# A quarter of a graph network's column terms from bf16 matmuls over runs of sorted edges instead of an indirect gather

## The reference

```python
for l in range(N_LAYERS):                      # 3
    f1 = relu(x[row] @ nb_W[l] + nb_b[l])
    f2 = relu(x[col] @ self_W[l] + self_b[l])
    h = relu(concatenate([f1, f2], axis=1) @ att1_W[l] + att1_b[l])
    log_alpha = (h @ att2_W[l] + att2_b[l])[:, 0]
    mask = clip(sigmoid(log_alpha) * (ZETA - GAMMA) + GAMMA, 0.0, 1.0)
    rowsum = segment_sum(mask, row, num_segments=n) + 1e-06
    d_inv_sqrt = clip(rowsum ** (-0.5), 0.0, 10.0)
    vals = mask * d_inv_sqrt[row] * d_inv_sqrt[col]
    x = segment_sum(vals[:, None] * x[col], row, num_segments=n)
    out = out + x
return layernorm(x_in + out)
```

## Time and profile before

| | us |
|---|---|
| median of 3 runs | 12785.2 |
| lowest, highest | 12784.3, 12812.13 |
| span of the profiled execution | 9111.0 |
| attention stage of one layer (669 to 2740) | 2071 |
| weight stage of one layer (2800 to 3425) | 625 |

### The profile page before, as it was taken

One profiled execution on the slowest core, in us unless ns is written; L12 is line 12 of the kernel. 1 busy time (PEld: TensorE's weight loads), 2 busy tenths in 40 slices (PEclk: granted clock), 3 DMA queues, 4 the chain that ended last, 5 costly groups with the idle time before them and its releaser, 6 DMA issues.

```text
span 9111.0 us, 203370 instructions
## 1 busy us (share of the span) xinstructions
PE 5650.8 (62%) x43467; PEld 5151.5 (57%) x43630; DVE 6736.5 (74%) x29039; ACT 3666.1 (40%) x8663; POOL 5960.7 (65%) x6294
## 2 busy tenths in 40 slices
PE   3135555555558996555555557998555555555996
PEld 1135555545548885555555556887555555555886
DVE  8877777777777877777777777877777777776788
ACT  0013322322227883322322325885322322323886
POOL 0017777777775656777777776665777777776664
PEclk7565555555558996555555557998555555555998
DMA  1014444444456664444444446665444444445665
GB/s 24 0 48 135 132 130 131 132 130 130 133 128 206 213 206 130 132 131 130 132 130 131 132 130 176 210 212 156 132 130 130 133 130 131 132 130 146 213 211 161
DMA packets 1122388, 1272.27 MB, mean 140 GB/s; under 512 B 648596, under 2 KB 652724, under 8 KB 1122356
## 3 DMA queue, kind: packets, MB, share of 16 engines
q1 hardware_dynamic: 922676, 903.51, 32.1%
q0 software_dynamic: 199680, 368.45, 16.7%
HBM read 868.11 MB, written 403.23 MB: 140 GB/s over the span
## 4 chain that ended last, share of the span: by engine, by line
POOL 44%; issue 23%; PE 22%; DVE 8%; DMA 1%; ACT 1%; POOLq 0%; DVEq 0%; ACTq 0%; SPq 0%
POOL got L526 22%; PE bank L552 12%; POOL k_hot L526 11%; POOL g_hot L526 10%; PE bank L685 6%; DVE acc L946 2%; DVE acc L947 2%; PE bank L653 1%; PE bank L690 1%; PE bank L610 1%; PE bank L601 1%; PE bank L576 1%; DMA k_x<-kept_x 1%; DMA k_hot<-qx_table,index 0%; DVE acc L909 0%
## 5 line engine op out<-in xcount | busy, mean ns | idle before, releaser
L653 PE MATMUL bank<-p_all,onehot_t 128*128 x10032 | 2301.5, 424 | 1752.4 <-issue 1731.8
L653 PEld LDWEIGHTS bank<-p_all,onehot_t 128*128 128x128 f32 x10032 | 2186.8, 330 | 1803.4 <-issue 1803.4
L526 POOL DMA_INDIRECT got<-qx_table,index x2496 | 2376.4, 952 | 784.9 <-issue 780.3
L539 POOL DMA_INDIRECT got<-y_table,index x1248 | 1187.3, 951 | 798.8 <-issue 431.5
L798 ACT ACTIVATE small<-small 128x8 f32<-128x8 f32 x624 | 130.2, 209 | 3813.9 <-DVE small L1080 3813.9
L526 POOL DMA_INDIRECT k_hot<-qx_table,index x1248 | 1181.3, 947 | 393.7 <-issue 377.5
L526 POOL DMA_INDIRECT g_hot<-qx_table,index x1248 | 1185.6, 950 | 380.6 <-issue 380.6
L552 PE MATMUL bank<-mask,onehots 128*128 128x3 bf16 x4992 | 669.8, 184 | 986.1 <-DVE mask L1091 986.1
L552 PEld LDWEIGHTS bank<-mask,onehots 128*128 128x128 bf16 x4992 | 516.0, 104 | 1250.7 <-issue 1145.5
L1118 DVE SCALAR_TENSOR_TENSOR p_all<-iota_b,col_hi,bank 128x104 f32<-128x104 bf16 x3768 | 953.9, 317 | 341.5 <-PE bank L685 335.4
L1056 DVE TENSOR_SCALAR onehots<-iota_b,rows_b 128x128 bf16<-128x128 bf16 x5016 | 888.7, 280 | 48.0
(11 more groups left out here) (167 smaller groups left out, 8859.7 us busy)
## 6 DMA issues: line engine op xcount, KB each, us to landing
onehot_t<-look_hot SPq DMA_DIRECT2D x474, 256.0 KB
row_hot<-onehots SPq DMA_DIRECT2D x468, 256.0 KB, 3.6
k_x<-col_rows SPq DMA_DIRECT2D x318, 256.0 KB, 3.6
kept_x<-got SPq DMA_DIRECT2D x312, 256.0 KB
look_hot<-k_x SPq DMA_DIRECT2D x312, 256.0 KB, 2.1
hot_in<-row_hot SPq DMA_DIRECT2D x312, 256.0 KB
k_x<-kept_x SPq DMA_DIRECT2D x312, 256.0 KB
look_new<-row_hot SPq DMA_DIRECT2D x159, 256.0 KB
```

The lines of the kernel that those rows point to most:

```text
L526: pool.indirect_dma_start(got[j][:, k, :], None, qx_table, bass.IndirectOffsetOnAxis(ap=index[j][:, k:k + 1], axis=0)).then_inc(a_got[j], 16)
L539: pool.indirect_dma_start(got[j][:, k, 0:HID], None, y_table, bass.IndirectOffsetOnAxis(ap=index[j][:, k:k + 1], axis=0)).then_inc(g_got[j ...
L653: last = mm(bank_p[h][:, k, :], onehot_t[h][:, k, :], p_all[:, ds(ids[k], 1), :].rearrange("p o d -> p (o d)"), start=True, stop=True)
```

## The change

One group in four, j = 3 of each quad, no longer gathers q. All edges are sorted by column too (the key is now block, column, row), so that a tile is a few runs of edges from the same column block, and for each run a bf16 one-hot over 128 columns times the block of q gives all of the run's terms. q is kept as three bf16 parts (`q3`, in the storage of `acc`) whose sum is q, so that a product has 192 columns. A quad has 72 such run slots: 9 rounds of 8. A round's one-hot is 128x1024 bf16; the rounds r % 3 < 2 are made by DVE in one compare (`build_slots`), every third by ACT in two activations (`make_third`). Two buffers hold them, `slot_hot[r % 2]`, and a buffer is free when PE has used the round two before (`x_used`). SP broadcasts each round's lane numbers from DRAM, 256 KB, into one of three buffers.

```diff
 # SP, quad loop
+                        if j == 0:
+                            sp.wait_ge(x_used[0], l * (slots_used(0) * QUADS) + b * slots_used(0))
+                            sp.dma_start(slot_word[0:1, :], slot_words[ds(b, 1), 1, :]).then_inc(w_in, 16)
+                            for r in range(3):
+                                load_slots(b, r, 0 if r == 0 else None)
...
+                        if j < 2:
+                            for r in (3 * j + 3, 3 * j + 4):
+                                load_slots(b, r, r - 2)          # waits until round r - 3 is made
...                                                               # kept_x store, look_hot store (waits a_look[j])
+                        if j < 2:
+                            load_slots(b, 3 * j + 5, 3 * j + 3)
 # POOL, quad loop: 3 groups in place of 4
-                    for j in range(4):
+                    for j in range(3):
...
+                pool.memset(acc[:, :, :], 0.0).then_inc(k_zero, 1)   # was 14 ACT copies per layer
 # PE
+                def column_terms(b, j):
...
+                    for r in range(3 * j, 3 * j + 3):
+                        pe.load(q_at + k_at, slot_word[0:1, 2 * U * r:2 * U * (r + 1)])   # 16 int32 registers
+                        pe.wait_ge(*slots_made(l, b, r))
+                        for i in range(U):
+                            of = pe.snap(q_at[i], min_val=0, max_val=(NB - 1) * Q_COLS)
+                            to = pe.snap(k_at[i], min_val=0, max_val=(U - 1) * OUT_COLS)
+                            last = plus(bank_q[:, ds(to, Q_COLS)], slot_hot[r % 2][:, i * PARTS:(i + 1) * PARTS],
+                                        q3_flat[:, ds(of, Q_COLS)])
+                        last.then_inc(x_used[r % 2], 1)
+                    for j in range(4):
+                        g = b * 4 + j
+                        if j == 2:
+                            column_terms(b, j)
+                            row_terms(1, g + 1)                  # into the same banks as the column terms
+                        else:
+                            row_terms(1 - j % 2, g + 1, a_sum, l * GROUPS + g)
+                        turn_hot((j + 2) % 4, g + 2)
+                        if j == 0:
+                            pe.wait_ge(a_sum, l * GROUPS + g)
+                            for i in range(4):
+                                clear(bank[4 + i])
+                        if j < 2:
+                            column_terms(b, j)
...                                                               # then the row sums, as before
 # ACT
+                def make_third(b, j):
+                    third, h, n = 3 * j + 2, j % 2, l * (3 * QUADS) + (b * 3 + (j + 1))
+                    act.wait_ge(x_in[2], n * 16)
+                    a.activation(slot_in[2], slot_in[2], ACT.Abs, bias=minus_part[:, :]).then_inc(x_away, 1)
+                    act.wait_ge(x_used[h], l * (slots_used(h) * QUADS) + (b * slots_used(h) + third // 2))
+                    act.wait_ge(x_away, n)
+                    a.activation(slot_hot[h], slot_in[2], ACT.Relu, bias=one[:, :], scale=-1.0).then_inc(x_third, 1)
                         a.activation(small[j % 2][:, 1, :], small[j % 2][:, 7, :], ACT.Exp, scale=-1.0).then_inc(a_sig, 1)
+                        if j == 2:
+                            make_third(b, j)
                         keep_turned(j % 2, g + 2, g + 1)
                         if j < 3:
                             make_look(b, j)
+                        if j < 2:
+                            make_third(b, j)
 # DVE
+                def build_slots(b, r):
+                    h = r % 2
+                    dve.wait_ge(x_in[r % 3], ...)
+                    dve.wait_ge(x_used[h], l * (slots_used(h) * QUADS) + (b * slots_used(h) + r // 2))
+                    v.tensor_scalar(slot_hot[h], slot_in[r % 3], part_f[:, :], None, ALU.is_equal).then_inc(x_made, 1)
-                        build_hot(hot_a[h], ...)                 # cast, 8 compares
+                        if j < 3:
+                            build_slots(b, 3 * j)
+                            build_slots(b, 3 * j + 1)
+                        build_hot((j + 2) % 4, g + 2, g, b + (j >= 2))   # one build_onehot of 128x1024, bf16
                         dve.wait_ge(a_p, l * (GROUPS + 1) + (g + 1))
-                        v.tensor_tensor(bank_p[h], bank_p[h], got[j][:, :, 0:HID], ALU.add)
+                        # j < 3: the same add; j == 3:
+                            v.tensor_reduce(terms, q_parts[:, :, 0:Q_COLS].rearrange("p k (s d) -> p k d s", s=PARTS_OF),
+                                            AX.X, ALU.add).then_inc(a_parts, 1)
-                        build_hot(hot_b[1 - h], ...)             # the second set of row one-hots
 # DVE, give_columns, per node step
+                    v.tensor_copy(q3[:, of_step(s), 0, :], q_out).then_inc(q_hi, 1)
+                    v.tensor_tensor(q_rest[j], q_out, q3[:, of_step(s), 0, :], ALU.subtract).then_inc(q_left, 1)
 # ACT: a copy per node step (split_middle); POOL: q3 part 2 = q_rest - q3 part 1
```

More of the change, by code:

```diff
@@ L206, in build @@
         onehots = sb("onehots", [PARTS, 4 * U, PARTS], BF16)
-        hot_a, hot_b = ([onehots[:, h * U:(h + 1) * U, :] for h in (first, first + 1)] for first in (0, 2))
+        hot = [onehots[:, j * U:(j + 1) * U, :] for j in range(4)]
         onehot_t = ring("onehot_t", [PARTS, U, PARTS], F32)
@@ L212, in build @@
                   .rearrange("p (k m) -> p k m", m=PARTS) for c in range(3)]
[L213 removed]
+        index = [sb(f"index{h}", [PARTS, U], I32) for h in range(3)]
         hidden = ring("hidden", [PARTS, U, HID], F32)
@@ L574, in _ @@
                 of = keys[stages_before(n) % 2]
+                if n == TURNS - 1:
+                    pe.wait_ge(s_ranked, 1)
+                    for h in range(2):
+                        last = turn(bank[7][:, h * PARTS:(h + 1) * PARTS], other[:, h * PARTS:(h + 1) * PARTS], ident_f[:, :])
+                    last.then_inc(s_kk, 1)
+                    of = other
+                    pe.wait_ge(s_perm, 16)
+                    pe.wait_ge(s_lo, 1)
                 for c in range(COLS // PARTS):
@@ L985, in _ @@
                     n += 1
-            done, free = keys[n % 2].bitcast(I32), keys[(n + 1) % 2].bitcast(I32)
-            link(v.tensor_scalar(free, done, PARTS - 1, None, ALU.bitwise_and))
-            v.tensor_copy(col_lo, free).then_inc(s_lo, 1)
+            done, moved = sorted_of.bitcast(I32), other.bitcast(I32)
+            own, real, group_key, runs, rank, first, rest, few, kk = (ranks[:, k, :] for k in range(9))
+            link(v.tensor_scalar(moved, done, HI_AT, None, ALU.logical_shift_right))
@@ new lines, in _ @@
+            link(v.tensor_tensor(starts[:, 1:COLS], moved[:, 1:COLS], moved[:, 0:COLS - 1], ALU.not_equal))
+            link(v.memset(starts.rearrange("p (t e) -> p t e", e=PARTS)[:, :, 0:1], 1.0))
+            link(v.tensor_reduce(runs, starts.rearrange("p (h e) -> p h e", h=2), AX.X, ALU.add))
+            link(v.scalar_tensor_tensor(out=kk, in0=runs, scalar=float(ALL_GROUPS), in1=group_key, op0=ALU.mult, op1=ALU.add))
+            v.tensor_copy(other[:, 0:ALL_GROUPS].rearrange("p (h m) -> p h m", h=2),
+                          kk.unsqueeze(2).to_broadcast([PARTS, 2, PARTS])).then_inc(s_ranked, 1)
@@ new lines, in _ @@
+            dve.wait_ge(s_kk, 1)
+            for h in range(2):
+                c.mark(v.tensor_scalar(starts[:, h * ALL_GROUPS:(h + 1) * ALL_GROUPS], bank[7][:, 0:ALL_GROUPS],
+                                       kk[:, h:h + 1], None, ALU.is_lt))
+            c.wait(dve)
+            link(v.tensor_reduce(rank, starts[:, 0:2 * ALL_GROUPS].rearrange("p (h e) -> p h e", h=2), AX.X, ALU.add))
+            v.tensor_scalar(first, rank, 4.0, 3.0, ALU.mult, ALU.add)
+            v.tensor_scalar(few, rank, float(QUADS), None, ALU.is_lt)
@@ new lines, in _ @@
+            link(v.tensor_scalar(rest, rank, -float(QUADS), 0.0, ALU.add, ALU.max))
+            link(v.tensor_scalar(ranks_i[:, 0, :], rest, 171.0, None, ALU.mult))
+            link(v.tensor_scalar(ranks_i[:, 1, :], ranks_i[:, 0, :], 9, None, ALU.logical_shift_right))
+            link(v.tensor_tensor(rest, rest, ranks_i[:, 1, :], ALU.add))
+            link(v.tensor_tensor(first, first, rest, ALU.subtract))
+            link(v.tensor_tensor(first, first, few, ALU.mult))
+            link(v.tensor_tensor(rest, rest, own, ALU.subtract))
@@ new lines, in _ @@
+            link(v.memset(run_start.rearrange("p (t e) -> p t e", e=PARTS)[:, :, 0:1], 1.0))
+            link(v.tensor_tensor(run_by, run_val, iota_e, ALU.add))
+            pair = [starts[:, 0:GROUP_EDGES], run_by]
+            link(v.tensor_tensor(pair[0], run_by, run_start, ALU.mult))
+            for r in range(ROUNDS):
+                eight = picks[:, 0, r * U:(r + 1) * U]
+                link(v.max(eight, pair[r % 2]))
```

(8 more changed lines are left out.)

394 lines of the change are left out of this document (284 added, 110 removed).

## The result

The kernel before takes 12784.75 us (median of 4 runs, 12775.13 to 12812.13), the changed one 14371.23 us (4 runs, 14347.64 to 14384.22): 1.1231 times as long, 95% interval 1.1214 to 1.1249. Forecast were 13790 us and a range of 12900 to 14700; +1003 us was expected, +1586 measured.

A forecast was written before the change was run, and what follows sets the result against it. POOL's indirect DMAs were taken to bound the kernel, then a chain through the run slots: +858 us for quads, +100 prologue, +45 node stage, +1003 on 12785, say 13790 us; range 12900 to 14700.

The forecast's parts named there:

- A: Time between the logit sums of groups j = 0 and j = 1 of a quad, through the run slots: 11.6 us.
- B: Time between the logit sums of groups j = 1 and j = 2: 11.6 us, or about 14.0 at 1.2 GHz.
- C: Time between the logit sums of groups j = 2 and j = 3: 12.0 us at 1.2 GHz, 10.2 at 2.4.
- D: From j = 3 to the next quad's j = 0: 10.2 us, including a 3.2 us wait for slot broadcasts.
- The clock: taken in the middle: TensorE's clock in the attention stage: a quad of 45.5 us, between 43.2 at 2.4 GHz and 47.8 at 1.2.
- The register loads priced at 0: TensorE's 16-register load per round, 0.6 to 1.2 us, costs 0 in links A and B, hidden under ACT's work.
- rival 4: Far slower: a load of 16 registers costs 4.4 us in TensorE's rounds, 17140 us in all; chance 0.06.
- under ScalarE's 5.8 us: Cover for the round's register load, issued before the slot wait; if it fails, 3.6 us a quad.
- the landing: In link D, the DMA time for slot broadcasts to arrive: 3.6 us, with 2.5 and 5.0 also considered.
- Prologue and node stage: Added work outside the attention stage: prologue +100 us (70 to 160), node stage +45 us (10 to 90).
- The 3674 us carried over unchanged: The median of the runs stands 3674 us above the profile's span of 9111; this was added to the new span unchanged.
- Rival 2: Faster: the 3674 us belong to indirect DMAs costing 0.59 us more each than the profile shows, 10840 us; chance 0.07.

The follow-up runs named there:

- e5: The changed kernel, unchanged, run again in a call where the kernel before took 9100 us: 11101 us, 1.220 times the kernel before.
- e6: The changed kernel with fixed addresses, without loads of 16 registers or register operations per product (column terms go to wrong edges): 10358 us.
- e11: The kernel before, unchanged, profiled again in a call with late instructions: 12808 us, span 12806.6.
- e3: The changed kernel with every third one-hot set made by VectorE and TensorE's three rounds of a group as an inner loop: 12477 us, 1.3705 times the kernel before.
- e2: The changed kernel with every third set of run one-hots made by VectorE, ScalarE's activations gone: 10447 us, 1.148 times the kernel before.
- e12: The changed kernel with all run one-hots by VectorE and fixed addresses without register loads, instructions in time: 8998 us, 0.989 times the kernel before.

## Why the prediction was right, and where it was not

**The bound moves off POOL to a chain through the run slots: right where instructions are in time.** In e5 POOL waits for its index, VectorE for the slots' buffers and TensorE for ScalarE's third, all three as named, and POOL has 1% of the chain. The sign "a quad of 43 to 48 us" failed in both conditions (51.7 and 63.7). In the condition of the result POOL was not the bound to begin with. Against the condition of rows 1 to 9 the links came out so, in us:

| link | forecast at 2.4 / 1.2 GHz | measured (e5) |
|---|---|---|
| A | 11.6 / 11.6 | 11.5 |
| B | 11.6 / 14.0 | 14.4 |
| C | 10.2 / 12.0 | 13.8 |
| D | 9.8 to 10.2 | 12.1 |
| quad | 43.2 / 47.8, taken 45.5 | 51.7 |

**The clock: taken in the middle, is low.** 0.55 over the stage, and no row term runs at the upper level (mean of one 424 ns, as in the kernel before): 47.8 was the number to take, 2.3 of the missing 6.2 us. The middle between the two levels had no row behind it.

**The register loads priced at 0: wrong.** A load of 16 takes 1.11 us (median of 1404), inside 0.6 to 1.2, so rival 4 is out. But the cover, "under ScalarE's 5.8 us", holds for the third round of A and B only. The sum of link C goes from ScalarE's third straight to round 8, but TensorE is still in round 7 when the third is ready, and then loads. C is 1.8 us over the forecast, and e6 takes 2.9 off it. In all e6 gives 4.8 us a quad, more than the 3.6 named for the case that the cover fails. By the figure of the Trainium skill ("Runtime: NRT & Kernel Launch", Instruction fetch mechanics), about 200 ns per register, a load would be 3.2 us, an estimate; the trace disagrees with its 1.11.

**Link D**: the landing was right, 3.79 us from the issue at 2070.53 to slot 0 at 2074.32. Sized too small were SP's steps ahead of it, 2.2 us from the end of the look-up one-hots to that issue where 1.05 were counted, and the second slot's broadcast, which VectorE awaits another 1.0 us. Together 2.2 in this quad; the link stands 1.9 over the forecast.

The issue rows of e5 in link D:

```profile
2068.48 0.37 SPq L543 DMA_DIRECT2D look_hot<-look_new  x1
2069.64 0.28 SPq L524 DMA_DIRECT2D slot_word<-slot_words  x1
2070.53 0.89 SPq L509 DMA_DIRECT2D hot_in<-slot_lanes  x2
2074.32 0.49 DVE L1366 TENSOR_SCALAR k_hot<-hot_in,part_f 128x1024 bf16<-128x1024 bf16 x1 [3.90 <-DMA hot_in<-slot_lanes]
2075.84 0.49 DVE L1366 TENSOR_SCALAR k_hot<-hot_in,part_f 128x1024 bf16<-128x1024 bf16 x1 [1.03 <-DMA hot_in<-slot_lanes]
```

**Single operations**: one-hot of slots 0.49 (0.55 taken), wide compare 1.22 (1.2), reduction 1.76 (1.8), a round's products 1.46 (1.5), third 1.13 + 1.15. All bounds from the nearest rows held.

**Prologue and node stage**: +100 and +45; measured +107 up to the first logit sum (which holds one node stage) and +20 per layer between. The sum of the two, 145, against 160 in all.

**The 3674 us carried over unchanged: wrong.** They lie inside the span of the runs, in every stage, and the change turned two stretches per quad into one. The prediction's alternative, all stages 1.40 times as long, gives 14190 and was nearer, for a reason that holds for the kernel before: its attention stages are 1.37 times as long and its weight stages 1.7. The changed kernel is only 1.30 times as long. Rival 2 put the time on indirect DMAs; a gather takes 947 ns in e11 (median of 2496), 0.95 in the earlier trace rows, and it is TensorE's, VectorE's and SP's instructions that are late (SP's start 0.70 to 0.74 or 1.39 to 1.42 us apart from 3037 to 3053 us of the changed kernel's trace).

**How the two errors met.** In the condition of the trace the sum should have been +2002, not +1003; of the 999 missing, 967 are the quad's 6.2 us. The late instructions took 416 back. The quad of the trace's condition, 51.7, lies above the upper bound of 50.5, and 12785 + 2002 = 14787 us would have been above the range. That the time lies inside it is luck: an error in the chain and one in the carried 3674 us had opposite signs.

## What to carry to other kernels

When two engines hand work back and forth in a short ring of buffers, write each engine's program order as one stream and add up everything in it, register loads too: a price of 0 needs a cover in every place where the instruction stands, not in one. Two waits that cover each other are worth little when one is removed (654 and 743 us) and more together (2104, with a higher clock in it); test the pair before giving up. And where a span and its runs differ by more than a few us, the profile describes another condition than the times: take a second profile before carrying the difference over.

## What the runs showed of the hardware

- One program takes 9100 or 12800 us with nothing changed, on one and the same chip in two calls. Where it is long, instructions of TensorE, VectorE and SP start 0.70 us (or a multiple) apart in stretches of some 9 to 15 us, at the rate of TensorE's loop; the weight stage takes 1080 us, not 625, with the clock at 0.74, not 0.99. Why a call is of the one or the other kind stays open.
- A load of int32 registers on TensorE: 0.59 us for 8, 1.11 for 16. Moving the row term's load from int16 to int32 took it from 2.2 to 0.6.
- At 1.2 GHz products of 192 columns start 0.16 us apart, with register offsets (e5) or fixed addresses (e6). At 2.4 GHz it is 0.147 with two loaded offsets and 0.083 with fixed addresses: the register operation hides at the lower clock and takes nearly all that the upper one would give. With one more register operation per product (e3) it is 0.26 at either.
- The granted clock of an attention stage was 0.57 in e2 and 0.67 in e12: part of the time at 2.4 GHz, as the row terms of 1.99 us in e12's timeline show beside the 3.67 of e5's. Nine loads are 10.0 us of TensorE's stream; the quad fell by 9.3, with the higher clock's gain in it.
